# Weighing the experts' outputs in feature rows, one tile later, and turning only their sum, in two mixture-of-experts stages

## The reference

```python
# stage 0, input x = layernorm(h)
gate_scores = einsum('bsd,ed->bse', x, Wg) + bg
topk_scores, topk_idx = top_k(gate_scores, 2)
combine = sum(softmax(topk_scores)[..., None] * one_hot(topk_idx, 8), axis=-2)
for e in range(8):
    hid = relu(einsum('bsd,hd->bsh', x, W1[e]) + b1[e])        # 256 wide
    out = out + combine[..., e:e+1] * (einsum('bsh,dh->bsd', hid, W2[e]) + b2[e])
h = h + out
# stage 1, flat = rmsnorm(x): probs = softmax(flat @ router_w.T), its two largest
# divided by their sum are the weights
for e in range(8):
    hh = silu(flat @ w1[e].T) * (flat @ w3[e].T)               # 170 wide
    out = out + weights[:, e:e+1] * (hh @ w2[e].T)
result = x + out
```

## Time and profile before

| | |
|---|---|
| median of three runs | 1119.44 us (1119.05 to 1119.71) |
| the profiled execution's span, first to last instruction | 1120.4 us |
| PE busy | 1041.2 us (93%) |
| DVE busy | 856.0 us (76%) |
| ACT busy | 610.7 us (55%) |
| POOL busy | 446.2 us (40%) |
| mean granted PE clock | 0.978 of full |
| stage 0, from its first up product | 224.3 to 538.1 us |
| stage 1, from its first up product | 769 to 1120.4 us |
| up products (line 1522), both stages | 1976 products, 621 us busy, overlapping |
| DMA | 15.6 MB in the whole run |

### The profile page before, as it was taken

The page is one execution under the profiler, slowest core; times in us unless marked ns, Lnnn a source line. Parts: engine busy times, 40 slices in busy tenths (PEclk is TensorE's granted clock), DMA queues, the critical chain, the costliest instruction groups (busy, mean ns, idle before and its releaser), DMA issues. The chain is left out here.

```text
span 1120.4 us, 24166 instructions
## 1 busy us (share of the span) xinstructions
PE 1041.2 (93%) x8747; PEld 764.9 (68%) x8747; DVE 856.0 (76%) x2048; ACT 610.7 (55%) x1321; POOL 446.2 (40%) x595
## 2 busy tenths in 40 slices
PE   6897889699999999999888799988999999999996
PEld 2475756477777777776665477755777777777774
DVE  2786959867777777778877589956788888888876
ACT  2375645565665555566337567755554554455452
POOL 3224402304443444434357577800244333344433
PEclk9898999989999999999989999999999999999999
DMA  8200000000000000000001000000000000000000
GB/s 230 126 1 2 2 1 2 1 1 1 1 1 1 1 1 2 1 1 1 1 24 42 8 2 2 3 2 1 1 7 7 13 8 7 7 8 7 7 7 12
DMA packets 5236, 15.56 MB, mean 14 GB/s; under 512 B 608, under 2 KB 3936, under 8 KB 4736
## 3 DMA queue, kind: packets, MB, share of 16 engines
q1 hardware_dynamic: 4784, 9.97, 3.1%
q0 software_dynamic: 336, 4.07, 0.9%
HBM read 11.91 MB, written 2.13 MB: 13 GB/s over the span
## 5 line engine op out<-in xcount | busy, mean ns | idle before, releaser
L1522 PE MATMUL moe_psU<-moe_nT_parts,moe_w_hi 128*128 128x320 f32 x988 | 324.5, 339 | 4.5 <-DVE moe_hid L1425 2.3
L1522 PE MATMUL moe_psU<-moe_nT_parts,moe_w_lo 128*128 128x320 f32 x988 | 296.5, 310 | 0.0
L1522 PEld LDWEIGHTS moe_psU<-moe_nT_parts,moe_w_hi 128*128 128x128 f32 x988 | 187.5, 190 | 60.6 <-issue 50.3
L1522 PEld LDWEIGHTS moe_psU<-moe_nT_parts,moe_w_lo 128*128 128x128 f32 x988 | 188.4, 191 | 0.0
L1419 DVE TENSOR_TENSOR moe_hid<-moe_psU,moe_silu 128x320 f32<-128x320 f32 x286 | 139.1, 491 | 49.8 <-ACT moe_silu L1193 40.7
L1093 POOL TENSOR_TENSOR moe_sum<-moe_scaled 128x256 f32<-128x256 f32 x124 | 93.5, 754 | 161.7 <-DVE moe_scaled L1409 161.4
L1193 ACT ACTIVATE moe_silu<-moe_psU 128x320 f32<-128x320 f32 x286 | 125.4, 439 | 56.1 <-PE moe_psU L1522 39.2
L1198 ACT ACTIVATE moe_hid<-moe_psU,middle 128x320 f32<-128x320 f32 x260 | 129.4, 527 | 30.9 <-PE moe_psU L1522 28.9
L1425 DVE TENSOR_SCALAR moe_hid<-moe_psU,middle 128x320 f32<-128x320 f32 x156 | 85.5, 549 | 55.8 <-PE moe_psU L1522 54.9
L1533 PE MATMUL moe_psY<-moe_hid,late 128*64 128x320 f32 x832 | 123.4, 439 | 0.9 <-DVE moe_hid L1419 0.9
L1533 PE MATMUL moe_psY<-moe_hid,middle 128*64 128x320 f32 x832 | 123.4, 439 | 0.7 <-ACT moe_hid L1198 0.7
(11 more groups left out here) (356 smaller groups left out, 1932.2 us busy)
## 6 DMA issues: line engine op xcount, KB each, us to landing
images<-in_x SPq DMA_DIRECT2D x8, 576.0 KB, 11.1
late<-in_late POOLq DMA_DIRECT2D x1, 2263.5 KB, 11.3
out_tokens<-h SPq DMA_DIRECT2D x13, 160.0 KB, 1.8
middle<-in_middle POOLq DMA_DIRECT2D x1, 1554.0 KB, 6.9
project_turns<-in_turns SPq DMA_DIRECT2D x8, 160.0 KB, 2.2
early<-in_early SPq DMA_DIRECT2D x1, 1043.0 KB, 19.0
turns_first<-in_turns SPq DMA_DIRECT2D x4, 160.0 KB, 2.5
turns_first<-in_turns POOLq DMA_DIRECT2D x1, 160.0 KB, 11.5
```

Source lines behind the costliest of these rows:

```text
L1522: last = pe.matmul(psum[:, 0:HALF], w[:, col:col + SPLIT], moving, start=(part == 0), stop=(part == 1))
```

## The change

The down products are no longer copied and turned one by one. Their weights are turned instead: PE turns the 40 routing weights of a tile (`turn_shares`, one turning), ACT copies them (`read_shares`), SP stores them in DRAM (20 KB), and loads them again eight times, each expert's 5 x 128 weights replicated to 64 partitions, so that `share` has a weight for each element of `psY`. DVE's `weigh` now reads `psY` itself, pair by pair, 640 columns, multiplied with `share` (stage 0: bias added in the same instruction). POOL adds the four pairs' `y`, 640 columns at a time (`add_pairs`), and only the sum is turned by PE (`turn_out`, five turnings), copied by ACT (`read_out`) and added to the residual by POOL, two adds of 320 columns (the two sides of a pair).

All this comes one tile later: the down groups of tile g - 1 run in body g, each at the end of the same pair's up products (`DOWN`), and the sum of tile g - 2 is turned in body g. The ring of `hid` has five pairs instead of two. What is left over comes behind the last body: PE does the four down groups of the last tile, two of them in the idle `psU` banks, and DVE does the last tile's sums and adds.

The places move: routing and norm steps (`SLOTS`) come ahead of the weighing at a pair's end and after units 1 or 2; `HI`, `KEEP`, `EXP` and `TURN` move with them. `gate_bank` is unchanged.

The diff, cut to its core:

```diff
-        hid_of = [units[u][0] % 2 * 8 + u - first_of[units[u][0]] for u in range(UPG)]
+    RING = PAIRS + 1
+        place = (g * PAIRS + p) % RING
...
-            need(eng, down_mm, g * PAIRS + (units[u][0] - 1))
+            need(eng, down_mm, (g - 1) * PAIRS + units[u][0])
...
-            LOGITS, DOWN = (0, 2), 4
-            OUTS = [(0, 7), (1, 2), (1, 7), (2, 2), (2, 6)]
-            TURN = [(3, 2)]
-            WEIGH = [(0, 7), (1, 3), (1, 7), (2, 3), (2, 7)]
-            HI, KEEP, EXP = (1, 5), [(3, 2)], (3, 0)
+            LOGITS, DOWN = (0, 2), (7, 7, 7, 7)
+            OUTS, READS = [(1, 0)], [(1, 1)]
+            SHARES, SHARES_READ = (3, 1), (3, 2)
+            TURN, KEEP = [(3, 4)], [(3, 4)]
+            HI, EXP = (2, 0), (2, 3)
-            SLOTS = {(0, 4): "aannnnnn", (1, 4): "naaaaaa", (2, 4): "naaaaaaa", (3, 4): "eeeeee"}
+            SLOTS = {(0, 7): "aaaannnn", (1, 2): "nn", (1, 7): "aaaaaaan", (2, 2): "aaa", (2, 7): "neeeeee"}
         else:
-            LOGITS, DOWN = (0, 0), 1
-            OUTS = [(0, 3), (1, 0), (1, 3), (2, 0), (2, 2)]
+            LOGITS, DOWN = (0, 0), (5, 5, 3, 5)
+            OUTS, READS = [(1, 0), (1, 3)], [(1, 1), (1, 4)]
+            SHARES, SHARES_READ = (3, 0), (3, 0)
             TURN = [(3, 1), (3, 3)]
-            HI, KEEP, EXP = (1, 3), [(3, 1), (3, 3)], (0, 3)
+            HI, EXP = (2, 0), (1, 0)
-            SLOTS = {(0, 1): "aaaannn", (1, 1): "neeeeee", (2, 1): "neeeeee", (3, 1): "eeeeeee"}
+            SLOTS = {(0, 5): "aaaannn", (1, 1): "ee", (1, 5): "neeeeeee", (2, 1): "eee", (2, 3): "neeeeeee"}
...
+                def add_pairs(j):
+                    need(pool, out_mm, j * PARTS)
+                    pool.wait_ge(weighed, j * PAIRS + 2)
+                    pool.tensor_tensor(y_sum[:, :], y[:, 0, :], y[:, 1, :], ALU.add).then_inc(summed, 1)
+                    for p in (2, 3):
+                        pool.wait_ge(summed, j * SUMS + (p - 1))
+                        pool.wait_ge(weighed, j * PAIRS + (p + 1))
+                        pool.tensor_tensor(y_sum[:, :], y_sum[:, :], y[:, p, :], ALU.add).then_inc(summed, 1)
...
+                for g in range(NT):                      # pool
+                    if g < NT - 1 or ahead:
+                        deviation(g + 1)
...
+                    if g >= 2:
+                        add_up(g - 2)
+                    if g >= 1:
+                        add_pairs(g - 1)
...
+                for g in range(NT):                      # sync
+                    if layer == 1 and g >= 2:
+                        store(g - 2)
+                    for p in range(PAIRS):
+                        need(sp, share_in[p], 32 * (g - 1))
+                    sp.wait_ge(shares_set, g + 1)
+                    sp.dma_start(shares[g % 2].rearrange("t e b -> (t e) b"), share_T[:, :]).then_inc(shares_kept, 16)
+                    sp.wait_ge(shares_kept, 16 * (g + 1))
+                    for p in range(PAIRS):
+                        need(sp, weighed, (g - 1) * PAIRS + (p + 1) if g else 0)
+                        for side in range(2):
+                            sp.dma_start(share[64 * side:64 * side + 64, p, :].rearrange("d (t b) -> d t b", b=B),
+                                         shares[g % 2][:, 2 * p + side, :].unsqueeze(0).to_broadcast([64, T, B])).then_inc(share_in[p], 16)
...
-                def read_y(g, slot, p):
+                def read_out(j, part, last=False):
+                    act.copy(y_out[:, t0:t1, :].rearrange("b t n -> b (t n)"),
+                             psM[:, 0:(t1 - t0) * 2 * D]).then_inc(out_read, 1)
+                def read_shares(g):
+                    act.copy(share_T[:, :], psM[0:T * E, SHARES_AT:SHARES_AT + B]).then_inc(shares_set, 1)
...
-                def weigh(g, t, ending=False):
+                def weigh(j, p, last=False):
+                    dve.wait_ge(down_mm, j * PAIRS + (p + 1))
+                    dve.wait_ge(share_in[p], 32 * (j + 1))
+                    need(dve, summed, (j - 1) * SUMS + max(p, 1) if j else 0)
+                        if layer == 0:
+                            ins = dve.scalar_tensor_tensor(into, psum, late[:, c["b2"]][:, p:p + 1], by, ALU.add, ALU.mult)
+                        else:
+                            ins = dve.tensor_tensor(into, psum, by, ALU.mult)
...
                     for p, k, u in places():         # dve
                         evict(g, u)
                         for kind in SLOTS.get((p, k), "") + ...
                                 next(work[kind], None)
+                        if g and k == DOWN[p]:
+                            weigh(g - 1, p)
...
+                        if g and k == DOWN[p]:           # tensor
+                            down(g - 1, p)
+                        for part in range(PARTS):
+                            if g >= 2 and (p, k) == OUTS[part]:
+                                turn_out(g - 2, part)
+                        if (p, k) == SHARES:
+                            turn_shares(g)
+                        for part in range(PARTS):
+                            if front and (p, k) == TURN[part]:
+                                transposes(g + 1, part)
...
+                body(NT - 1)
+                down(NT - 1, 0, True)
+                pe.wait_ge(shares_set, NT)
+                for part in range(PARTS):
+                    turn_out(NT - 2, part)
+                for p in range(1, PAIRS):
+                    down(NT - 1, p, True)
```

More of the change, by code:

```diff
@@ L938, with over_bodies, moe @@
 TOP_TWO_LINKS = 11
-def over_bodies(eng, body, chain=None, per=0):
-    def counted(start, steps, call):
+def over_bodies(body, chain=None, per=0):
+    for g in range(NT - 1):
         if chain is not None:
-            chain.enter(start, steps * per)
-        call()
-    counted(0, 1, lambda: body(0, 0, False, True))
-    if chain is not None:
-        chain.leave(1)
-    for g in range(1, NT - 1):
-        counted(0, 1, lambda: body(g, g % 2, True, True))
+            chain.enter(0, per)
+        body(g)
         if chain is not None:
             chain.leave(1)
-def moe(nc, layer, late, early, src, resid, out, minus_half, first, ahead=None):
+def moe(nc, layer, late, early, src, resid, out, minus_half, first, shares, ahead=None):
     c, ec = columns(LATE if layer else MIDDLE)[0], columns(EARLY)[0]
@@ L1140, in _ @@
                 if layer == 1:
-                    with sp.Fori(0, NT) as g:
-                        sp.wait_ge(added, g + 1)
-                        sp.dma_start(out[:, bass.ds(g * T, T), :], resid[:, bass.ds(g * T, T), :]).then_inc(stored, 16)
+                    store(NT - 2)
+                    store(NT - 1)
                     sp.wait_ge(stored, 16 * NT)
@@ new lines, in down, with turn_out @@
+                    ins.then_inc(down_mm, 1)
+                def turn_out(j, part, last=False):
+                    t0, t1 = (0, T) if last else TURNS[part]
+                    pe.wait_ge(summed, (j + 1) * SUMS)
+                    if part == 0:
+                        pe.wait_ge(L_read, min(j + 3, NT))
+                        need(pe, out_read, j * PARTS)
+                    else:
+                        pe.wait_ge(out_read, j * PARTS + part)
+                    for t in range(t0, t1):
+                        ins = pe.transpose(turned_ps(t, last), y_sum[:, t * B:(t + 1) * B], ident)
+                    ins.then_inc(out_mm, 1)
@@ L2296, in program @@
                     if phases > 2:
-                        moe(nc, 0, middle, early, h, h, None, minus_half, first, ahead)
+                        moe(nc, 0, middle, early, h, h, None, minus_half, first, shares, ahead)
                 if phases > 3:
@@ L2302, in program @@
             if phases > 5:
-                moe(nc, 1, late, early, n_all, h, out, minus_half, first)
+                moe(nc, 1, late, early, n_all, h, out, minus_half, first, shares)
 def resize_matrix(n):
```

313 lines of the change are left out of this document (149 added, 164 removed).

## The result

| | before | after |
|---|---|---|
| median (range) | 1119.58 us (1119.05 to 1121.28, 4 runs) | 1147.42 us (1142.47 to 1150.35, 4 runs) |
| span of the profiled execution | 1120.4 us | 1146.0 us |
| stage 0, one tile | 22.95 us | 24.38 us, some of 26.07 |
| stage 1, one tile | 26.20 us | 26.30 us |

The ratio is 1.0223, with a 95% interval of 1.0189 to 1.0257. The forecast was 1131 us, with a range of 1102 to 1144. The direction was right; of the rise only 11.5 of 27.8 us were foreseen.

What follows compares the result with a forecast made beforehand. PE's issue was taken to bound both expert stages. Stage 0's tiles +10, stage 1's -4 and the ends +5.5 gave +11.5 us on 1120.4, with the median 1 us lower: 1131 us, own range 1122 to 1144, whole down to 1102.

Steps and rivals of the forecast that it cites:

- The floors: PE's own work per tile after saving 1.54 us of turnings: 21.4 us in stage 0, 24.7 in stage 1.
- routing steps at unit 2 of pair 2: Stage 0: a DVE step waits for POOL's long add, delaying unit 3's eviction and PE's unit 7; 1.4 us lost a tile.
- weighing 1 late: Stage 0: two residual adds under the steps ahead make weighing 1 some 0.4 us late, costing 0.3 more a tile.
- ACT's copy of the shares: Stage 0, pair 3: ACT copies after evicting unit 2, so PE's turning after unit 4 stalls 0.3 us a tile.
- The clock: At the two stage ends a granted clock at half would add up to 7 us; kept for the range only.
- Stage 0's tail: Behind stage 0's last up product: much the same as stage 1's +7.1, taken as +6.5 us.
- The bank's repeat: Stage 1, unit 2 of pair 2 reuses unit 1's gate bank: 0.6 us of stall, 0.9 with weighing 1's lateness.
- The ends: First tiles save 3 and 4 us, tails add 6.5 and 7.1 for three more down groups; +5.5 us after turnings.
- Shares by DMA: SP's queue: a store and eight loads, priced from a 2.2 us load, stay hidden with 2.7 us over; cost nothing.
- late-shares rival: From 2.7 us a load weighings wait for shares; at 3.3 us a load the total is 1221 us; chance 0.06.
- POOL's adds do not bite: Rival: DVE steps slip between POOL's adds; 22.6 and 25.3 us a tile, 1110 or 1104 us; chance 0.25.
- PE's floor is reached: Rival: both stages' tiles save the full 1.54 us, 24 times; -31.5 us in all, 1088 us; chance 0.09.

Runs made afterwards that it cites:

- the last edit: Against the kernel joining all order and bank edits (1106.58 us): in stage 0, three routing steps moved from unit 7, pair 1 to unit 3, pair 2; 1095.50 us.
- experiments 4 with the bank alone: Changed kernel with stage 1's immediate repeat of a gate bank moved from unit 2 to unit 0 of pair 2: 1145.75 us, ratio 1.0216.
- 5: Changed kernel with ACT's part of the next stage's work put ahead of reading out tile NT-2 in stage 0's last body: 1142.48 us, ratio 1.0194.
- 6: Changed kernel with each load of shares, from a stage's second tile on, bringing 128 columns instead of 640: 1148.38 us, ratio 1.0252.
- 3 with norm steps or share copy alone: Changed kernel, stage 0: either norm steps moved behind unit 3's eviction in pair 1, 1144.63 us, or ACT's share copy one unit earlier, 1135.16 us.
- experiments 1 and 2: Changed kernel with POOL's first add waiting for the third weighing, 1132.78 us; or with POOL's adds cut to 64 columns in most tiles, 1132.73 us.

## Why the prediction was right or wrong

**The floors** were right to 0.0 in stage 0 (21.4 forecast, 21.40 reached) and 0.4 short in stage 1 (24.7, 25.13). Both stand in windows without idle, so the 1.54 us a tile of removed turnings were real: 22.95 - 21.40 = 1.55. In stage 1 it was 1.07; what takes the other 0.4 was not measured.

**Stage 0's stalls, forecast 2.4 us a tile, measured 24.38 - 21.40 = 2.98.** The first step that failed is this list, by its terms:

| term of the sum | forecast | measured | by |
|---|---|---|---|
| routing steps at unit 2 of pair 2 | 1.4 | 1.39 | moved alone |
| weighing 1 late, put down to the adds to the residual | 0.3 | 0.89 | 22.29 to 21.40, the last edit |
| norm steps at unit 2 of pair 1 | 0.4 | 0.13 | moved alone |
| ACT's copy of the shares | 0.3 | 0.59 | moved alone |

The size that decided was in the second term. The forecast let the two adds delay weighing 1 by 0.4 us together. In the trace each catches one step (L933 to 0.85, L935 to 0.91), 0.65 + 0.71 = 1.4 us. A rule that had been applied in full to the long add was applied to the short ones by feel. The last edit also takes three steps away from ahead of weighing 1, so it prices the lateness and not the adds alone. In the kernel that it starts from, the adds hold L930 and L931 (0.61 and 0.91 us, so 1.12 more than 0.20 each), and weighing 1 starts 1.10 us behind the end of its down group (369.58 and 368.48): by the rows the adds are enough to make all of it, but no run took them away alone. The first term, 1.4 for 1.39, was right in its working as well as in its number; the third was too high, which hid a part of the other two. In the fourth term the forecast's 1.2 us from unit 2's start to the end of the copy was right (408.51 to 409.75 in the tile shown), but PE starts 0.26 us after the copy ends (410.01), and that was left out. And an idle in a timeline is less than its cost: the product ahead of it is shown 0.31 us long (from 409.33) where the next could have started after 0.15, at 409.48, so the 0.38 of idle is 0.53 lost.

**The clock.** The second step that failed: the forecast kept the granted clock's fall for the range, and for the ends alone. It came inside the tiles. In the six kernels with the idle of 1.13 us in pair 2 (the changed one and experiments 4 with the bank alone, 5, 6, and 3 with norm steps or share copy alone), 12 of 66 whole tiles of stage 0 have a down group of 4.0 to 4.1 us and are 1.7 us longer; in the seven kernels without it, none of 77. In the changed kernel that is 3 x 1.7 = 5.1 us, with a third such group in the last body (523.52). Why one tile falls and its neighbour with the same idle does not was not found. Stage 0's tiles missed by 7.3 us: these 5.1, and 12 x 0.58 = 7.0 (a whole tile rose by 1.43 for 0.85), less 4.8: 0.6 in the second tile and 4.2 in the last body, of which 2.4 are a down group that was counted twice (see the ends).

**Stage 0's tail**, +13.5 against 6.5, is the third step that failed, and as large as the tiles: the forecast wrote "Stage 0 much the same" as stage 1, and did not follow ACT's queue there. Experiment 5 gives 6.1 of the 7.0 back, idle of 2.94 us and slow groups both. They have one cause: an order in which ACT's wait for a turning that PE does two down groups later stands ahead of work that others need.

**Stage 1** was right in the sum of its stalls (1.2 forecast, 26.30 - 25.13 = 1.17 measured; 25.9 forecast a tile, the missing 0.4 being the floor). Of its two stalls the trace shows the bank's as 0.9 us of idle a tile; the one at the turning of the shares shows in one of eleven whole tiles (0.31 us) and comes out in full only when the bank's is removed. So the argument of which one counts was too simple. The bank's repeat "0.6 of stall, 0.9 with the lateness" gives nothing when it is removed alone, and so does nearly POOL's add alone (0.19). PE waits for the later of two; the price of 0.89 is paid to both.

**The ends.** First tiles -4.1 and -1.7 where -3 and -4 were taken; stage 1's tail 6.2 for 7.1. The last body of a stage got 1.1 and 3.2 us shorter; the forecast had counted it as a whole tile, +0.85 and -0.35. That is an error of counting. "The end gains three down groups" is not what the change does: in both stages PE had four groups ahead of the last up product and one behind it, and has three and five now (stage 0's fourth group stood at 520.97, ahead of the last up product at 524.11, and stands at 536.65 now, behind that of 536.42). The forecast's tail of 18.4 us has all five in it, and the last body was still priced with four, so about 2.4 us stand twice in each stage. In stage 1 this hid by luck about half of what the tiles had too much, 0.45 us each.

**Shares by DMA**: 4.4 us a load and not 2.2, over the 2.7 at which the late-shares rival was to begin. Yet no weighing waited for a load. That threshold had the eight loads one behind the other. SP's queue shows them side by side:

```profile
385.07 5.22 SPq L1163 DMA_DIRECT2D moe_share<-shares  x8
```

All eight are issued in 5.22 us, so by an estimate from these rows (5.22 + 4.4) the last is in less than 10 us after the first was issued, where eight of 4.4 us in a row would be 35 us, more than a tile. So the row for a load was wrong by a factor of two, and the rule that they follow one another was wrong too, the other way; the conclusion held, for a reason that was not the one given. The load of the earlier trace rows has the same size but another shape; whether it is the shape or the company of seven others that makes 4.4 of 2.2 us was not measured.

**Rivals.** "POOL's adds do not bite" fell by experiments 1 and 2. What the forecast says "decides" is whether DVE passes the steps at unit 2 of pair 2 before weighing 1 has released POOL: it does not, L933 starts 0.42 us after the add (401.40 and 400.98). "PE's floor is reached" is what the last kernel does inside its tiles; in time it reached 1095.5 us for the rival's 1088. (The chances by direction, 0.36 and 0.56, are not the sums of those by case, 0.34 and 0.58.)

## What to carry to other kernels

When an instruction on one engine is made longer (here POOL's add from 0.86 to 1.55 us), list every instruction of its partner that can stand beside it, and what is queued behind each; put chains of small steps behind the eviction that PE waits for next, not ahead of it. Price every member of such a list by the same rule, the short ones too, and follow each queue through the tail of a stage, where the order of the loop no longer holds. When taking away one of two waits gives nothing, take away both before calling it free.
